# Ten of 32 scan pairs write their states to SBUF, and GpSimd makes their product with C

## What is computed

```
dA  = exp(einsum('bld,dn->lbdn', delta, A))
dBu = einsum('bld,bln,bdl->lbdn', delta, B, u)
def step(carry, inp):
    a, bu, c = inp
    carry = a * carry + bu
    y = einsum('bdn,bn->bd', carry, c)
    return carry, y
...
y = y + u * D
y = y * silu(res)          # then the output projection
x = layernorm(x + attn);  x = layernorm(x + ffn(x))
```

## Time and profile before

| | us |
|---|---|
| three runs: median (lowest to highest) | 2986.29 (2984.62 to 2989.06) |
| the profiled execution, its time | 2989.11 |
| the profiled execution, its span | 2987.1 |

### The profile page before, as it was taken

The page is one execution under the profiler, slowest core; times in us unless marked ns, Lnnn a source line. Parts: engine busy times, 40 slices in busy tenths (PEclk is TensorE's granted clock), DMA queues, the critical chain, the costliest instruction groups (busy, mean ns, idle before and its releaser), DMA issues. The chain is left out here.

```text
span 2987.1 us, 36784 instructions
## 1 busy us (share of the span) xinstructions
PE 2517.6 (84%) x12290; PEld 1881.9 (63%) x12290; DVE 2529.1 (85%) x2497; ACT 2186.1 (73%) x3335; POOL 1394.2 (47%) x1476
## 2 busy tenths in 40 slices
...
GB/s 55 252 307 194 176 185 208 194 207 196 208 199 195 207 194 208 192 210 193 194 203 195 208 190 212 196 209 202 189 202 186 209 194 211 197 199 200 224 114 116
DMA packets 230128, 584.84 MB, mean 196 GB/s; under 512 B 26017, under 2 KB 26401, under 8 KB 229809
## 3 DMA queue, kind: packets, MB, share of 16 engines
...
## 5 line engine op out<-in xcount | busy, mean ns | idle before, releaser
L793 DVE TENSOR_TENSOR_SCAN scan_ps<-dA,scan_ps 128x1024 f32<-128x1024 f32 x512 | 1170.5, 2286 | 124.8 <-PE scan_ps L387 123.6
L972 POOL DMA_DIRECT2D y<-hC x512 | 452.1, 883 | 1180.7 <-DVE hC L803 1137.8
L387 PE MATMUL scan_ps<-ident,dB 128*128 128x128 f32 x4096 | 586.9, 290 | 243.9 <-DVE hC L803 220.2
L639 ACT ACTIVATE dB<-duT,bT 128x512 f32<-128x512 f32 x1024 | 724.7, 711 | 83.6 <-PE scan_ps L387 83.6
L387 PEld LDWEIGHTS scan_ps<-ident,dB 128*128 128x128 f32 x4096 | 497.4, 149 | 391.5 <-DVE hC L803 174.4
L630 ACT ACTIVATE dA<-delta,a_neg 128x512 f32<-128x512 f32 (+1 forms) x1024 | 710.2, 712 | 34.4 <-DVE hC L803 33.1
L803 DVE TENSOR_TENSOR hC<-scan_ps,c_rows_sb 128x1024 f32<-128x1024 f32 x512 | 622.8, 1216 | 94.8 <-DMA y<-hC 79.6
L501 PE MATMUL ffn_ps<-hb_hi,ring 128*128 128x512 f32 x1536 | 656.4, 427 | 34.6 <-POOL hb_lo L1011 24.2
L501 PE MATMUL ffn_ps<-hb_lo,ring 128*128 128x512 f32 x1536 | 612.9, 399 | 0.0
L501 PE MATMUL ffn_ps<-ha_hi,ring 128*128 128x512 f32 x1024 | 436.6, 426 | 4.1 <-POOL ha_lo L1011 4.1
L501 PE MATMUL ffn_ps<-ha_lo,ring 128*128 128x512 f32 x1024 | 402.8, 393 | 0.0
...
## 6 DMA issues: line engine op xcount, KB each, us to landing
y<-hC POOLq DMA_DIRECT2D x512, 512.0 KB, 5.7
...
c_rows_sb<-c_rows ACTq DMA_DIRECT2D x256, 256.0 KB, 4.0
...
x<-ffn_w SPq DMA_DIRECT2D x22, 512.0 KB, 10.6
...
```

The costliest lines, as they stand in the source:

```text
L387: mm = nc.tensor.transpose(dst[:, j * P:(j + 1) * P], src(j), ident[:])
L639: nc.scalar.activation(dB[:, n % 2, t, :], duT[:, t, :], ACT.Copy, scale=bT2[:, par, t, n:n + 1]).then_inc(dB_ready, 1)
L793: nc.vector.tensor_tensor_scan(b, dA[:, a:a + 2, :].rearrange("p a l -> p (a l)"), b, 0.0, ALU.mult, ALU.add).then_inc(scan_done, 1)
L972: pool.dma_start(y2[:, par, c:c + 2, :], hC[:, p % 2], accum_op=ALU.add).then_inc(y_added[p % 2], 16)
```

## The change

In the pairs 1, 4, 7, 10, 13, 17, 20, 23, 26 and 29 of each row (`POOL_PAIRS`) DVE's scan writes its states to a slot of `hC` in SBUF instead of back to PSUM, and DVE makes no product. POOL multiplies the slot by the C row in place and then starts the add as before. `hC` has four slots. `hC_done` becomes two counts, `hC_dve` and `hC_pool`. A scan or a product of pair p waits for the add of pair p-4. PE may fill the banks of a POOL pair again as soon as its scan is done. `load_c` waits for both counts. The area for POOL's DMA descriptors is halved, from 8,192 to 4,096 bytes. The new tuple `EXP_COUNT` holds the same numbers as the old formula gave.

```diff
+HC_SLOTS = 4
+POOL_PAIRS = (1, 4, 7, 10, 13, 17, 20, 23, 26, 29)
+ON_POOL = [p in POOL_PAIRS for p in range(PAIRS)]
+def products_upto(r, p, on_pool):
+    return r * sum(b == on_pool for b in ON_POOL) + sum(b == on_pool for b in ON_POOL[:p])
...
-        hC = sb("hC", [P, 2, 2, SEQ])
+        hC = sb("hC", [P, HC_SLOTS, 2, SEQ])
...
+        def wait_product(eng, r, p):
+            eng.wait_ge(hC_pool if ON_POOL[p] else hC_dve, products_upto(r, p + 1, ON_POOL[p]))
+        def wait_slot(eng, r, p):
+            g = r * PAIRS + p - HC_SLOTS
+            if g >= 0:
+                eng.wait_ge(y_added[g % 2], 16 * (g // 2 + 1))
...
-                wait_past(pe, hC_done, r * PAIRS + (p - 1))
+                g = r * PAIRS + p - 2
+                if g >= 0 and ON_POOL[g % PAIRS]:
+                    pe.wait_ge(scan_done, g + 1)
+                elif g >= 0:
+                    wait_product(pe, *divmod(g, PAIRS))
...
-                wait_past(act, hC_done, r * PAIRS + 2 * (n - 1))
+                last = r * PAIRS + 2 * (n - 1)
+                if last > 0:
+                    wait_past(act, hC_dve, products_upto(last // PAIRS, last % PAIRS, False))
+                    wait_past(act, hC_pool, products_upto(last // PAIRS, last % PAIRS, True))
...
-                nc.vector.tensor_tensor_scan(b, dA[:, a:a + 2, :].rearrange("p a l -> p (a l)"), b, 0.0,
+                if ON_POOL[p]:
+                    wait_slot(dve, r, p)
+                    states = hC[:, (r * PAIRS + p) % HC_SLOTS].rearrange("p a l -> p (a l)")
+                else:
+                    states = b
+                nc.vector.tensor_tensor_scan(states, dA[:, a:a + 2, :].rearrange("p a l -> p (a l)"), b, 0.0,
...
             def c_pair(r, p):
-                n, half = divmod(p, 2)
+                if ON_POOL[p]:
+                    return
...
-                pool.wait_ge(hC_done, r * PAIRS + (p + 1))
+                slot = (r * PAIRS + p) % HC_SLOTS
+                if ON_POOL[p]:
+                    n = p // 2
+                    pool.wait_ge(scan_done, r * PAIRS + (p + 1))
+                    pool.wait_ge(c_loaded[n % 2], r * (16 * STATES // 2) + 16 * (n // 2 + 1))
+                    nc.gpsimd.tensor_tensor(hC[:, slot], hC[:, slot],
+                                            c_rows[:, n % 2].unsqueeze(1).to_broadcast([P, 2, SEQ]), ALU.mult
+                                            ).then_inc(hC_pool, 1)
+                wait_product(pool, r, p)
...
-    nc = bacc.Bacc("TRN2", target_bir_lowering=False, num_devices=1, dynamic_dma_scratch_size=8192)
+    nc = bacc.Bacc("TRN2", target_bir_lowering=False, num_devices=1, dynamic_dma_scratch_size=4096)
```

More of the change, by code:

```diff
@@ L102 @@
 EXP_LEAD, DA_RING = 4, 8
-NO_EXP = {s % TILES for s in GELU_AT}
-EXP_COUNT = [0 if s in NO_EXP else 1 for s in range(TILES)]
-for s in sorted(NO_EXP):
-    EXP_COUNT[max((k for k in range(s) if 0 < EXP_COUNT[k] < 3), key=lambda k: (EXP_COUNT[k] == 1, k))] += 1
+EXP_COUNT = (2, 2, 0, 0, 1, 1, 1, 2, 0, 1, 1, 1, 1, 1, 1, 1, 1, 1, 1, 1, 1, 1, 1, 1, 1, 1, 1, 1, 1, 1, 1, 1, 1, 1, 1, 1, 2, 2, 0, 0, 1, 1, 1, 1, 2, 2, 0, 0, 2, 2, 0, 0, 1, 2, 2, 2, 0, 0, 0, 1, 1, 1, 1, 1)
 EXP_FIRST = EXP_LEAD
@@ L792, in scan_pair @@
                 b = scan_ps[:, h:h + 2, :].rearrange("p a l -> p (a l)")
[L793 removed]
+                if ON_POOL[p]:
[4 more added lines that the diff above has]
+                nc.vector.tensor_tensor_scan(states, dA[:, a:a + 2, :].rearrange("p a l -> p (a l)"), b, 0.0,
                                              ALU.mult, ALU.add).then_inc(scan_done, 1)
             def c_pair(r, p):
[L797 removed]
+                if ON_POOL[p]:
+                    return
+                n = p // 2
                 h = 2 * (p % 2)
[L799 to L801 removed]
+                dve.wait_ge(c_loaded[n % 2], r * (16 * STATES // 2) + 16 * (n // 2 + 1))
+                wait_slot(dve, r, p)
                 dve.wait_ge(scan_done, r * PAIRS + (p + 1))
[L803 removed]
+                nc.vector.tensor_tensor(hC[:, (r * PAIRS + p) % HC_SLOTS], scan_ps[:, h:h + 2, :],
                                         c_rows[:, n % 2].unsqueeze(1).to_broadcast([P, 2, SEQ]), ALU.mult
[L805 removed]
+                                        ).then_inc(hC_dve, 1)
             def front_step(r, par, s, tail):
```

14 lines of the change are left out of this document (3 added, 11 removed).

## The result

| us | before | after |
|---|---|---|
| median of four runs (lowest to highest) | 2987.03 (2984.62 to 2989.06) | 3028.06 (3020.21 to 3033.6) |
| profiled execution: time, span | 2989.11, 2987.1 | 3020.21, 3017.7 |

The change makes the kernel slower by 1.5% (ratio 1.0149, 95% interval 1.0125 to 1.0174). 2961 us was forecast, with 2890 to 3020 us as the range. The profiled execution is the lowest of the four.

The account below looks back on a forecast made before the run. DVE was taken to set the pace in pairs 8 to 19, PE in 20 to 7. Per row -2.48 - 1.1 + 0.6 + 0.3 + 1.0 = -1.7 us, over 15 rows -25 us: 2961 us, range 2890 to 3020.

Parts of the forecast that it names:

- What bounds the kernel: DVE sets the pace in pairs 8 to 19, PE in 20 to 7; pairs 10, 13, 17 save 2.48 us a row.
- The new operation: POOL's product on 1024 elements takes 2.4 us, ends 2.25 and 2.57; the scan to SBUF stays at 2.286 us.
- DVE busy 195 us less: Sign to look for: DVE's busy time falls by 160 products of 1.216 us.
- Four slots: Products' waits for landed adds go; in PE's stretch, its wait for products saves 1.1 us a row.
- I take 0, ends 0 and 1.2 us: ACT's `load_c` waiting for POOL's product at pairs 1, 7, 13, 17 and 23: 0, at most 1.2 us.
- Pairs 1 and 4 at `ha`: Before the last `ha` tile: pair 1 absorbed, pair 4 1.6 us late, 1.3 hidden; +0.3 us, ends 0.2 and 1.8.
- Pair 23: Before five `hb` tiles: the last comes later and PE waits; +0.6 us a row, ends 0.4 and 2.57.
- Nothing by themselves: Products taken off DVE at pairs 20, 23, 26, 29, 1, 4 and 7, in PE's stretch, save nothing.
- Pair 26: At DVE's two-input SBUF operations, POOL's product holds DVE up, delaying du: +1.0 us a row, ends -0.5 and +1.8.
- 25 us better: Without the rule that POOL and two-input DVE operations block one another, pair 26 gains and the sum improves 25 us.
- POOL becomes what PE waits for: Rival: `hb`, `ha` and du come later, 6.9 us against 3.6 of gains; +3.3 us a row, 3036 us; chance 0.27.
- The signs named beforehand: Expected waits and operation times, and disproofs: POOL's product over 3 us, PE's stretch over 2 us shorter, PE's POOL waits past 4.

Follow-up runs that it names:

- pair 28: Kernel with only pairs 10, 13 and 17 on POOL, plus pair 28, three to four steps behind the softplus: 2943.72 us, against 2929.99 without it.

## Why the prediction was wrong, step by step

- **What bounds the kernel: right.** The stretch of pairs 8 to 19 went from 70.9 to 68.85 us; 2.48 us were forecast for the three pairs, 2.05 came in the row shown and 1.9 in the mean. With three pairs only, the same sum gave 2933 us and 2930 was measured.
- **The new operation: right**, 2.39 us in the median where 2.4 stood, and the scan to SBUF 2.280 us against 2.288. In the softplus shown it took 2.86 us, and 3.24 at most, once in 160.
- **DVE busy 195 us less: wrong in form.** The products' 194 us are gone, but the time in which DVE is held up counts as busy: the two groups of L868 and the two of L874 hold 158.6 us against 109.2.
- **Four slots: -1.1 us a row forecast, -0.5 measured.** The row gained 1.85 us from the softplus to the gate tile and lost 1.0 up to the first result of `w3`, with 0.3 lost ahead of the softplus; DVE's waits for the gate tile rose from 37.2 to 72.6 us.
- **`load_c`: "I take 0, ends 0 and 1.2 us". This is the step that failed.** The queue was named, and the gate tile behind it too (the list of pairs lacked 29). What was wrong is the end of the range: it priced the wait at the difference of two products, as if POOL began when DVE would have. POOL began 6.4 us after the scan of pair 1 had ended (1501.2 to 1507.57), since an add that waited for another to land and two splits stood ahead of it. In the full list 2.2 us a row reach PE by the gate tile; with the `ha` wait and the clock pair 1 costs 3.5. Beside three pairs it costs 2.5 by another path, which is only in part explained.
- **Pairs 1 and 4 at `ha`: +0.3 forecast, 2.2 for pair 4 alone**, above the upper end of 1.8. The 1.6 us later was about right (1.8 measured), and so, by luck, was the size of the cover: 1.1 us were hidden, at another place than the one named. What was put at nothing is the clock: PE's matmuls behind the wait ran at the lower level in 10 of 13 rows, 1.1 us a row.
- **Pair 23: +0.6 at `hb` was right, its effect 0 by the medians and -0.5 by the rows.** DVE, with a product less, reached the softplus 1.55 us earlier, and that was worth at least as much. "Nothing by themselves" for the pairs in PE's stretch was too strict the other way.
- **Pair 26: +1.0 forecast, +1.9 measured**, upper end 1.8. Half of it is the hold-up named: L874 on gate 2.11 us instead of 0.71. The other half would be there without any softplus (pair 28). The Trainium skill, "SBUF — State Buffer", section "Who interferes with whom", calls this an exclusive lock. By that rule, the trace agrees: POOL's product of 2.86 us lies inside two DVE operations of 4.57 us. The same section says that a DVE instruction with at most one SBUF input, outside the modes that use two ports, doesn't contend with GpSimd. The trace agrees there too: the 27 DVE products that ran beside a POOL product took 1.225 us and the others 1.217, the 57 scans 2.289 and the others 2.285. (The "25 us better" without the lock is a little high by the prediction's own numbers: from +1.0 to the lower end of -0.5 is 1.5 us a row, 22 us.)
- **The rival "POOL becomes what PE waits for"** gave 3036 us and came true in size, with a chance of 0.27. Its condition did too: the costs passed 3.6 us a row. But that was in part luck: it left out ACT's part, 2.2 us, and the clock, and had too much at `hb`.
- **The signs named beforehand.** "PE's waits for POOL past 4 us a row" did show: 54.4 + 38.0 us are 5.8 a row. DVE's waits for transposes grew as said, to 102.1 + 34.1 from 123.6 us. The sign that mattered, the gate tile, was not on the list.

The terms as measured, for a row: slots -0.5, pairs 10, 13 and 17 -3.1, pairs 7, 20 and 29 -0.55, pair 23 -0.5, pair 4 +2.2, pair 26 +1.9, pair 1 +3.5. Their sum is +3.0 us, and the row grew by 2.9. The forecast was -1.7. Of the 4.6 us between, pair 1 makes 3.5, pair 4 1.9, pair 26 0.9 and the slots 0.6; the other pairs gave 2.2 us more than forecast.
